# Five of GpSimd's eight scatters of a batch wait for later features

## The reference

```python
def reference(x, ...):                      # x: (8, 512, 256) float32
    xn = _layernorm(x)
    return x + attn(xn) + moe(xn)

def attn(x):                                # 16 heads of 16, 128 features each
    q, k, v = split(x @ W_qkv.T)
    q_p = elu(q @ proj) + 1;  k_p = elu(k @ proj) + 1
    kv = k_p^T v;  z = 1 / (q_p . sum(k_p) + 1e-8)
    return (q_p kv * z) @ W_out.T + b_out

def moe(x):                                 # 8 experts, the two best of each token
    weights = softmax(logits masked to the top 2 of x @ Wr + br)
    h = gelu(x @ W1[e] + b1[e]);  out = sum_e weights[e] * (h @ W2[e] + b2[e])
```

## Time and profile before

| | |
|---|---|
| median of 3 runs | 701.68 us (700.38 to 701.80) |
| the profiled execution's own time | 700.86 us |
| its span, first to last instruction | 698.7 us |
| PE busy | 682.9 us, 98% |
| DVE, ACT, POOL busy | 504.1, 475.3, 227.9 us |
| granted TensorE clock, mean | 0.996 |
| attention over the batches | to about 300 us, then the experts |
| one batch of the loop | 35.05 us |

### The profile page before, as it was taken

The page is one execution under the profiler, slowest core; times in us unless marked ns, Lnnn a source line. Parts: engine busy times, 40 slices in busy tenths (PEclk is TensorE's granted clock), DMA queues, the critical chain, the costliest instruction groups (busy, mean ns, idle before and its releaser), DMA issues.

```text
span 698.7 us, 17362 instructions
## 1 busy us (share of the span) xinstructions
PE 682.9 (98%) x5503; PEld 603.3 (86%) x5504; DVE 504.1 (72%) x1246; ACT 475.3 (68%) x875; POOL 227.9 (33%) x169
## 2 busy tenths in 40 slices
PE   8899999999999998999999999999999999999996
PEld 4666777777777776589999999999999999999996
DVE  8798888888888878748577675556777545577544
ACT  5687969696969696776557775447775444577553
POOL 2053232323232324643232532225233222322422
PEclk9999999999999999999999999999999999999999
DMA  8856474747474647765455663336556333454531
GB/s 266 200 182 170 108 228 106 228 106 228 106 228 106 198 106 223 224 189 142 100 98 118 145 167 46 46 47 106 178 71 167 48 52 53 81 131 107 69 48 23
DMA packets 87205, 91.65 MB, mean 131 GB/s; under 512 B 60049, under 2 KB 73361, under 8 KB 84897
## 3 DMA queue, kind: packets, MB, share of 16 engines
q1 hardware_dynamic: 71426, 59.36, 33.9%
q0 software_dynamic: 13872, 18.75, 15.2%
q10 hardware_dynamic: 1872, 13.11, 5.1%
HBM read 39.32 MB, written 26.67 MB: 94 GB/s over the span
## 4 chain that ended last, share of the span: by engine, by line
PE 82%; DVE 6%; issue 4%; ACT 2%; POOL 2%; DMA 2%; SPq 1%; POOLq 0%; DVEq 0%
PE F L527 9%; PE F L528 9%; PE F L529 9%; PE WK L527 5%; PE F L596 5%; PE WK L529 4%; PE WK L528 4%; PE NUM L527 4%; PE NUM L529 4%; PE NUM L528 4%; PE DEN L605 4%; PE DEN L527 4%; PE DEN L529 4%; PE DEN L528 4%; PE F L590 3%
## 5 line engine op out<-in xcount | busy, mean ns | idle before, releaser
L1932 POOL DMA_INDIRECT out<-ysb,icur x75 | 121.0, 1613 | 270.6 <-DVE ysb L1763 241.0
L1218 ACT ACTIVATE h<-F,b1c 128x384 f32<-128x384 f32 x200 | 112.2, 575 | 140.0 <-PE F L529 131.2
L1740 DVE TENSOR_TENSOR hl<-h,hh 128x768 fp32r<-128x768 f32 x100 | 96.1, 962 | 111.6 <-ACT hh L1222 111.6
L1063 ACT ACTIVATE e_ring<-F 128x512 f32<-128x512 f32 x256 | 145.7, 621 | 38.5 <-PE F L590 35.0
L527 PE MATMUL F<-gxh,wh 128*128 128x384 f32 (+1 forms) x400 | 128.6, 321 | 0.4 <-DVE wl L1641 0.4
L528 PE MATMUL F<-gxl,wh 128*128 128x384 f32 (+1 forms) x400 | 128.0, 320 | 0.0
L529 PE MATMUL F<-gxh,wl 128*128 128x384 f32 (+1 forms) x400 | 128.0, 320 | 0.0
L1866 POOL DMA_INDIRECT xg<-rows,slots x64 | 63.2, 988 | 174.0 <-PE F L590 158.8
L1468 DVE SCALAR_TENSOR_TENSOR kp<-F,e_ring 128x512 f32<-128x512 f32 x128 | 82.7, 680 | 13.2 <-PE DEN L605 6.2
L1468 DVE SCALAR_TENSOR_TENSOR qp<-F,e_ring 128x512 f32<-128x512 f32 x128 | 85.2, 683 | 8.5 <-ACT e_ring L1063 7.0
L1222 ACT ACTIVATE hh<-h 128x768 fp32r<-128x768 f32 x100 | 84.6, 846 | 3.3
(11 more groups left out here) (261 smaller groups left out, 1552.6 us busy)
## 6 DMA issues: line engine op xcount, KB each, us to landing
wraw<-experts ACTq DMA_DIRECT2D x12, 1024.0 KB, 6.2
gblk<-xg SPq DMA_DIRECT2D x100, 96.0 KB
Sk<-kdh SPq DMA_DIRECT2D x64, 128.0 KB, 2.3
Sq<-qdh SPq DMA_DIRECT2D x64, 128.0 KB
xin<-x SPq DMA_DIRECT2D x8, 512.0 KB, 5.5
Sk<-kdl SPq DMA_DIRECT2D x32, 128.0 KB, 2.4
Sq<-qdl SPq DMA_DIRECT2D x32, 128.0 KB
xres<-x SPq DMA_DIRECT2D x8, 512.0 KB
```

What stands on the lines that cost most here:

```text
L1063: A(e_ring[:, u % 4, :], F[u % 4][:, :], ACT.Exp, bias=EXP_BIAS, scale=1.0 / DOWN).then_inc(exp_done, 1)
L1218: A(h32[:, m, :], F[m % 4][:, 0:T], ACT.Gelu, bias=b1c[:, w, m:m + 1]).then_inc(gelu, 1)
L1740: V.tensor_tensor(hl[:, 2 * q:2 * q + 2, :], h32[:, 2 * q:2 * q + 2, :], f32(hh[:, 2 * q:2 * q + 2, :]), ALU.subtract).then_inc(hl_rdy, 1)
L1932: pool.indirect_dma_start(out, bass.IndirectOffsetOnAxis(icur[:, s, :], 0), ysb[:, s, :], None, bounds_check=last_token, compute_op=ALU.ad ...
```

## The change

In the loop and in batch 0, scatters 1 to 3 of a batch wait for `f_full` 1, 3, 5 as before, and scatters 4 to 8 for 13, 15, 17, 19, 21 instead of 7, 9, 11, 13, 15; that is for features 12, 14, 16, 18, 20 instead of 6, 8, 10, 12, 14. The last batch keeps the old numbers. The register `turn` is counted up by the differences of the new list.

```diff
     TURN = 2
+    TURNS = (1, 3, 5, 13, 15, 17, 19, 21)
...
             for n in range(NT):
                 for r in range(2):
+                    k = 2 * n + r
                     if isinstance(b, int):
-                        pool.wait_ge(f_full, 32 * b + 1 + TURN * (2 * n + r))
+                        pool.wait_ge(f_full, 32 * b + (1 + TURN * k if b == NB - 1 else TURNS[k]))
                     else:
                         pool.wait_ge(f_full, turn)
-                        pool.reg_add(turn, turn, TURN if n + r < NT else 32 - TURN * (2 * NT - 1))
+                        pool.reg_add(turn, turn, TURNS[k + 1] - TURNS[k] if k < 2 * NT - 1 else 32 + TURNS[0] - TURNS[k])
                     send_block(n, r, sent)
```

## The result

| | before | after |
|---|---|---|
| median | 701.74 us (700.38 to 701.91) | 712.86 us (711.99 to 714.49) |
| ratio, 95% interval | | 1.0176 (1.0161 to 1.0190) |
| span of the profiled execution | 698.7 us | 709.8 us |
| DVE busy | 504.1 us | 517.0 us |
| from the first scatter of batch 7 to the end | 432.0 us | 432.0 us |

The change makes the kernel 1.76% slower, 11.1 us. The prediction had the direction and the mechanism, but its 707.4 us is too small by half of the loss, and its range ended at 710.0.

The account below looks back on a forecast made before the run. PE was taken as the bound, without slack in loop batches. GpSimd's add and copy holding norm steps cost 1.3 us in five batches, 6.5 us on 700.86, giving 707.4 us; range 700.8 to 710.0.

Parts of the forecast that it names:

- What bounds the kernel: Loop batches: PE is busy 34.93 of 35.05 us, and VectorE has no slack against it at feature 27.
- the sum: Loop batches 1 to 5: holds delay feature 23 by 1.43 us; less 0.15 spare, PE loses 1.3 us a batch.
- Where the moved work goes: Loop batches: scatter 8 at 180.04, add 181.11 to 183.52, copy 184.51 to 185.55; waiting for them costs zero.
- The mechanism: Norm steps beside the moved add and copy: a two-SBUF-input VectorE instruction and a GpSimd SBUF reader wait for each other.
- rival 1: Loop batches: the tiny norm steps are not held, only DMA order changes; 700.4 to 701.8 us, chance 0.16.
- L1367 meets the add: Loop batches 1 to 5: L1367 is held to the add's end, 183.52 instead of 182.47; feature 21 is 0.73 late.
- the copy's share: Loop batches 1 to 5: L1369 starts inside the copy and ends at 185.55; feature 23 is 1.43 us late.
- the term for the steps from L1367 on: Batches 1 to 5: add and copy hold L1367 and L1369, costing PE 1.3 us each, 6.5 us in all.
- Rival 2: Loop batches: the add gets ahead of L1365 and holds it; 1.85 to 2.65 us a batch, 710 to 714, chance 0.14.
- near tie: Loop batches: L1365 begins 2.28 us after unit 20, the add 2.37, so only 0.09 us lie between.
- Rival 3: First half of a batch: fewer scatters let Sq stack and x load land earlier; at most 0.7 us, 700.2, chance 0.04.

Follow-up runs that it names:

- experiment 1: Changed kernel with the norm's nine VectorE steps moved to features 25 to 30: 702.09 us, ratio 1.0016; on the second chip kind 715.13 us, 0.9930.
- experiment 2: Kernel before, scatters early, with only the nine norm steps moved to features 25 to 30: 720.02 us, ratio 0.9998, on the second chip kind.
- experiment 3: Changed kernel with the bias add moved between the third and fourth scatter, copy still last: 718.99 us, ratio 0.9975, on the second chip kind.
- experiment 6: Changed kernel with GpSimd's copy ahead of the add, their order swapped: 712.91 us, ratio 1.0202 to the kernel before.
- Experiment 7: Changed kernel with the norm's aggregation and first two steps ahead of feature 17, plus one small added VectorE instruction: 706.41 us, ratio 1.0082.
- experiment 8: Changed kernel with only the eighth scatter late: norm steps late 700.73 us (1.0004); steps in old place 738.39 us (1.0250); scatter one feature pair earlier 726.27 us (1.0067).
- experiment 4: Changed kernel without any edit, run on the second chip kind beside the kernel before: 723.81 us, ratio 1.0042.

## Why the prediction was right and wrong

**What bounds the kernel**: right. PE lost all of VectorE's delay at feature 27 (2.79 late on VectorE, 2.80 on PE) and 2.70 by the end of the batch; the 0.15 us that the sum took as spare did not show at feature 27.

**Where the moved work goes**: right. Scatter 8 came 1.31 us behind feature 20 (1.30 forecast), the add 2.39 (2.37), the copy 3.9 to 4.6 behind scatter 8 (4.47). No engine but GpSimd itself, whose copy waits for the landing, waited for the add, the copy or the landing; batch 0 and the experts did not change, and batch 6 stayed within 0.1 us.

**The mechanism**: right, and shown by experiments 1 to 3. A VectorE instruction that meets GpSimd's add or copy waits until its end, even with four elements a partition. So rival 1 falls; `exm` in the earlier trace rows had met only the last 0.14 us of a copy and was no evidence, as the text said.

**The step that failed** is the opening of the sum, "L1367 meets the add": which instruction is the first to be held. It took L1365, and with it L1363, as safe since L1365 would begin "0.09 us" before the add, and since "no row shows such an instruction held by POOL". Both grounds were wrong:
1. An instruction with one SBUF input and a constant is held as fully as one with two. Steps 0 and 1 show it in two number types: 2.73 us and 3.05 us.
2. A start ahead of the add's row is no protection. The add is behind scatter 8 in GpSimd's queue, and from somewhere between 0.32 and 0.41 us after the scatter began, VectorE's instruction waits for the add (table in experiment 6). The window in which a step is caught is therefore not 2.41 us long but about 3.1.

So the first victim was step 0, two positions earlier than forecast; nearly the whole add fell on VectorE (2.57 us late at step 2, where the sum had 0), and the copy's share (2.79 - 2.57 = 0.22) was small: step 2 took 0.61 us more than usual, but the 0.30 us that VectorE had waited for ScalarE ahead of feature 21 are gone. The sum had 0.73 and 0.70 for the two. Experiment 7 puts the steps where the sum assumed them: its median is 6.3 us over before's on that chip, by the ratio 0.82% or 5.7 us, and its profiled batches are 0.9 us longer where the sum had 1.3 (4.4 us in five batches against 6.5). So the term for the steps from L1367 on was of the right size, by the batches somewhat high; what was left out was that steps 0 and 1 stand in the add's way, about 1.5 us a batch.

**Rival 2** described most of what came (it named L1365 as the first victim; it was L1363): held ahead of L1367, 1.85 to 2.65 us a batch, 710 to 714. Its feature 21 was to start 2.8 us late; it started at 154.18 instead of 151.37, 2.81 late; the batches are 2.18 to 2.70 us longer. It was given 0.14 on the ground of a near tie. A near tie of two engines, whose outcome decides 1 us a batch, should have had near to even chances, and the range should have reached to 714.

**Rival 3**: no gain on the first kind of chip (experiments 1 and 8 are at 1.0016 and 1.0004). On the second kind something of that sort exists, because PE has idle time there that the trace before did not show.

The Trainium skill ("SBUF — State Buffer", section Who interferes with whom) says that the engine that issues second waits for the whole of the first one's instruction, and that tensor_scalar may enter a mode which contends with GpSimd. The runs agree with the first: the holds end within 0.04 us of the add's or the copy's end. They agree with the second as far as tensor_scalar was held; in which mode it ran no run shows. They differ in what "first" means by the trace's rows: in experiment 4 VectorE's row begins 0.60 us ahead of GpSimd's, and VectorE still waits. The measurement decides.

## What to carry to other kernels

When work on one engine is moved, list not only who waits for it but what runs beside it at the new place, and take every small instruction near the border as caught, here from about 0.4 us into the issue of the scatter ahead of the mover. If a tie decides the price, price both sides at near even chances. Here the cheap remedy was to move the other side: nine VectorE instructions of 0.15 us each, placed one to six features later, took back 1.6 of 1.76%.

## What was unexpected of the hardware

- A VectorE instruction of 4 elements a partition can take 3.05 us, 0.6 of it before the GpSimd instruction that holds it has a row of its own.
- Two GpSimd instructions in direct succession can hold one VectorE instruction over both: 3.69 us, with 2.40 and 1.05 for the two.
- The issue of an indirect DMA itself held nothing: 0.19 to 0.20 us against 0.16.
- PE's idle time costs twice where the clock falls behind it, as in four of five batches of experiment 8. Experiment 6's second batch lasted 40.9 us in the same way: PE idle for 2.79 us up to 119.15, with a low granted clock in the windows around and behind it:

```profile
118.00:124.00 6.00, 4.85 (x16) 4.32 (x17) 5.02 (x19) 1.71 (x5) 0.47 (x1) 0.54 0.00 0
124.00:128.00 4.00, 4.00 (x22) 2.40 (x21) 1.91 (x6) 2.75 (x7) 0.00 (x0) 0.83 0.00 0
```

- One program takes 701 us on some chips and 720 us on others, and a change's ratio (1.0176 and 1.0042) goes with the kind. The cause stays open.
